# Writing out the last five slots, moving constant loads and border work

## What is computed

```python
x = _layernorm(x + _L0_attn_ref(x, ...))                 # linear attention with cos/sin features
x = _layernorm(x + _L0_xattn_ref(x, ctx_2048, lens, ...)) # rmsnorm, W_in, plus a table row per patch
x = _layernorm(x + _L0_ffn_ref(x, weight, bias))         # both operands rounded to 6-bit floats in blocks of 32
```

## Time and profile before

| | us |
|---|---|
| median of 3 runs | 1659.92 (1659.71 to 1660.7) |
| the profiled execution | 1660.41 |
| its span, first to last instruction | 1658.6 |
| mean granted clock, share of 2.4 GHz | 0.984 |

### The profile page before, as it was taken

How to read it: one execution, slowest core, us unless ns; L and a number is a source line. 1 busy time by engine, 2 the same in 40 slices (tenths; PEclk the granted TensorE clock), 3 DMA queues, 4 the chain that set the end, 5 groups by cost and what they waited for, 6 DMA issues and landing times. The chain is left out here.

```text
span 1658.6 us, 29661 instructions
## 1 busy us (share of the span) xinstructions
PE 1588.7 (96%) x11188; PEld 1122.3 (68%) x11188; DVE 1188.5 (72%) x1831; ACT 1115.1 (67%) x1454; POOL 711.1 (43%) x668
## 2 busy tenths in 40 slices
PE   6999999999999999999999999988699999999995
PEld 4756675676676667667666756754478888888884
DVE  5677667758757766875776676888587777777873
ACT  5597678668667767866876776678145656565654
POOL 2033105303411520440341053346178878897886
PEclk8999999999999999999999999999799999999998
DMA  4100202200210220220022022001612222222211
GB/s 169 52 26 1 78 1 78 77 1 26 77 52 1 77 77 2 67 86 2 2 77 77 1 78 77 27 26 51 162 32 83 83 77 83 82 84 78 74 52 51
DMA packets 49175, 95.75 MB, mean 58 GB/s; under 512 B 3552, under 2 KB 3872, under 8 KB 49056
## 3 DMA queue, kind: packets, MB, share of 16 engines
q1 hardware_dynamic: 38944, 76.29, 14.5%
q10 hardware_dynamic: 10112, 17.69, 2.9%
HBM read 60.38 MB, written 33.59 MB: 57 GB/s over the span
## 5 line engine op out<-in xcount | busy, mean ns | idle before, releaser
L764 DVE SCALAR_TENSOR_TENSOR feat<-feat,phases 128x1024 f32<-128x1024 f32 x256 | 300.8, 1216 | 177.0 <-ACT feat L657 176.9
L657 ACT ACTIVATE feat<-phases 128x1024 f32<-128x1024 f32 x256 | 248.3, 1024 | 147.1 <-PE phases L510 125.5
L664 ACT ACTIVATE feat<-feat 128x1024 f32<-128x1024 f32 x256 | 271.7, 1062 | 67.6 <-DVE feat L764 58.8
L383 POOL TENSOR_TENSOR xt_hi<-xt_raw,singles 128x512 fp32r<-128x512 f32 x60 | 69.0, 1180 | 526.6 <-PE bank L502 491.9
L670 ACT ACTIVATE feat<-feat 128x1024 f32<-128x1024 f32 x256 | 255.7, 1045 | 5.1 <-DVE feat L771 5.1
L771 DVE TENSOR_SCALAR feat<-feat 128x1024 int32<-128x1024 int32 x256 | 198.7, 780 | 45.7 <-ACT feat L664 45.1
L396 POOL TENSOR_TENSOR res<-res,bo_all 128x512 f32<-128x512 f32 x60 | 72.1, 1226 | 182.2 <-DMA res<-x 182.1
L598 PE MATMUL kv_sum<-feat,kv_cols 128*32 128x512 f32 x1024 | 124.3, 603 | 0.0
L572 PE MATMUL kv_sum<-feat,v 128*32 128x256 f32 x2048 | 123.8, 382 | 0.0
L500 PE MATMUL bank<-xt_hi,win_hi 128*128 128x512 f32 x256 | 108.7, 425 | 8.5 <-DVE win_lo L713 8.5
L1232 ACT ACTIVATE xs<-xs,shift,rstd 128x512 f32<-128x512 f32 x96 | 71.4, 806 | 67.3 <-POOL shift L1107 67.3
(11 more groups left out here) (204 smaller groups left out, 3678.7 us busy)
## 6 DMA issues: line engine op xcount, KB each, us to landing
normed<-res SPq DMA_DIRECT2D x32, 513.0 KB, 4.2
xt_raw<-xT SPq DMA_DIRECT2D x15, 1024.0 KB, 7.1
res<-x SPq DMA_DIRECT2D x30, 512.0 KB, 4.1
xs<-normed SPq DMA_DIRECT2D x24, 513.0 KB, 3.9
out<-xs ACTq DMA_DIRECT2D x24, 512.0 KB, 2.8
feat<-normed SPq DMA_DIRECT2D x8, 513.0 KB, 3.8
out<-feat ACTq DMA_DIRECT2D x8, 512.0 KB, 2.8
xt_raw<-ctx SPq DMA_DIRECT2D x8, 256.0 KB, 3.4
```

The lines of the kernel that those rows point to most:

```text
L657: act.activation(feat[2 * (w % 2) + p][:, 0, :], phases[:, 2 * p:2 * p + 2, :].rearrange("p h n -> p (h n)"), ACT.Identity, bias=ROUND).th ...
L664: act.activation(f[:, 1, :], f[:, 0, :], ACT.Sin, scale=-TWO_PI).then_inc(sin_done, 1)
L764: dve.scalar_tensor_tensor(f[:, 0, :], f[:, 0, :], ROUND, phases[:, 2 * p:2 * p + 2, :].rearrange("p h n -> p (h n)"), ALU.subtract, ALU.s ...
```

## The change

It has these parts:

1. SP issues the constant loads, after the weights and ahead of the second chunk of x. DVE makes `lens_f` in `weight_peaks`, near the end of the first part.
2. The DVE steps of the weight rounding stand one phase earlier (cos 2 to cos 7), and POOL runs `residual_weight` right behind `quantise_weight`, before the powers of that batch.
3. The powers have five steps. DVE makes one combined variance after the moments, the norm waits for the first power only, and the store waits for all.
4. The table of batch 0 is made in the first part: the new steps `context`, `table` and `parts` stand between the last output products.
5. In the second part `lin` and `ffn` do the eight matmuls with the high part first. They wait for ACT's high part, and only the last four wait for DVE's low part.
6. The last slots are a list of their own, `closing_steps`, with five slots. Slot 0 normalises the last pair alone, `ffn` results are normalised one slot later, the added bias is a step on POOL, and for the last pair DVE does the scaling and all of the rounding (`by_vector`).

```diff
@@ attention_steps, tail list
-        15: [..., norm(0, 0), norm(0, 1), ("ends",), W(1, 0),
-             ("repeats",), W(1, 1), W(1, 2), W(1, 3), stats(1), norm(1, 0), norm(1, 1)],
+        15: [..., norm(0, 0), norm(0, 1), ("ends",), W(1, 0),
+             ("repeats",), W(1, 1), ("context",), W(1, 2), W(1, 3), stats(1), ("table",), norm(1, 0), norm(1, 1), ("parts",)],
@@ SP
             def store(k, last=False):
+                sp.wait_ge(ln_step, LN_STEPS * (k + 1))
...
                         sp.dma_start(stage[m], w.rearrange("(k p) o -> p k o", p=P)).then_inc(w_in[m], 16)
+                    for to, of in const_loads:
+                        sp.dma_start(to, of).then_inc(const_in, 16)
                     load_xt(1)
@@ POOL, powers
-                pool.wait_ge(moments_done, k + 1)
-                step(1, pool.tensor_tensor(shifted, var, eps[:, 0, :], ALU.add))
-                step(2, pool.tensor_tensor(rstd, shifted, half_power[:, 0, :], ALU.pow))
...
+                pool.wait_ge(var_ready, k + 1)
+                pool.tensor_tensor(scale, spread_var, half_power[:, 0, :], ALU.pow).then_inc(ln_step, 1)
+                pool.tensor_tensor(shifted, var, eps[:, 0, :], ALU.add).then_inc(ln_step, 1)
+                pool.tensor_tensor(root, spread_var, half_power[:, 1, :], ALU.pow).then_inc(ln_step, 1)
+                pool.wait_ge(ln_step, base + 3)
+                pool.tensor_tensor(rstd, shifted, half_power[:, 0, :], ALU.pow).then_inc(ln_step, 1)
+                pool.wait_ge(ln_step, base + 4)
...
+                pool.tensor_tensor(res[:, :, RMS_COL:RMS_COL + 1]..., root, rstd, ALU.mult).then_inc(ln_step, 1)
@@ POOL, tail and last
-                    residual_weight(i - 1)
                     powers(2 * i - 2)
+                    pool.wait_ge(squared, 1)
+                    pool.tensor_tensor(shifted_square, mean_square, rms_eps, ALU.add).then_inc(context_scaled, 1)
+                    pool.wait_ge(context_scaled, 1)
+                    pool.tensor_tensor(context_inv, shifted_square, minus_half, ALU.pow).then_inc(context_scaled, 1)
                     powers(2 * i - 1, last=True)
...
                     quantise_weight()
+                    residual_weight(i)
                 powers(2 * i - 1)
@@ PE, ACT and DVE, the new steps of the first part
+                    elif kind == "table":
+                        pe.wait_ge(patch_ready, 1)
+                        pe.matmul(out_part[0], kept.decay[:], patch, start=True, stop=True).then_inc(table_done, 1)
...
+                    elif kind == "context":
+                        act.wait_ge(kept.context_in, 16)
+                        act.wait_ge(win_split, KD)
+                        act.activation(squares, context, ACT.Square, scale=DCTX ** -0.5, accum_out=mean_square).then_inc(squared, 1)
...
+                    elif kind == "context":
+                        dve.wait_ge(context_scaled, 2)
+                        dve.wait_ge(constants_in, 16 * 3)
+                        dve.scalar_tensor_tensor(patch, context[:, 0:D], context_inv, kv_cols[0:PATCHES, 1, :], ALU.mult, ALU.mult).then_inc(patch_ready, 1)
...
-            for to, of in const_loads:
-                act.dma_start(to, of).then_inc(const_in, 16)
...
-            dve.wait_ge(const_in, CONSTS)
-            dve.tensor_copy(lens_f[:], lens_i[:]).then_inc(lens_ready, 1)
@@ second part, first slot and closing slots
-            [("select",), ("turn", 0), ("patch",), ("count",), ("table",), ("choose",), ("turn", 1), ("means",), ("norms",)],
+            [("select",), ("turn", 0), ("count",), ("turn", 1), ("choose",), ("means",), ("norms",)],
...
+        [("quant", -3), ("lin", -1, 0), ("lin", -1, 1), ("means", 0), ("norms", 0), ("scale", -2), ("ffn", -4, 0), ("ffn", -4, 1),
+         ("back", -3, 0), ("back", -3, 1)],
+        [("bias", -3), ("quant", -2), ("means", 0), ("norms", 0), ("scale", -1), ("ffn", -3, 0), ("ffn", -3, 1),
+         ("back", -2, 0), ("back", -2, 1)],
+        [("bias", -2), ("means", 0), ("norms", 0), ("quant", -1), ("ffn", -2, 0), ("ffn", -2, 1), ("back", -1, 0), ("back", -1, 1)],
+        [("bias", -1), ("means", 0), ("norms", 0), ("ffn", -1, 0), ("ffn", -1, 1)],
+        [("means", 0), ("norms", 0)],
@@ PE, second part
-                        product(b[:], turn_hi[t], turn_lo[t], win_hi, win_lo, False)
+                        freed(last_use)
+                        wait(pe, hi_ready, i * hi_order.n + hi_place(mode, ("turn", k, t)) + 1)
+                        high_product(b[:], turn_hi[t], win_hi, win_lo)
+                        freed(place(mode, ("turn", k, t)))
+                        low_product(b[:], turn_lo[t], win_hi, False)
```

164 lines of the change are left out of this document (105 added, 59 removed).

## The result

The changed kernel takes 1649.55 us (median of 4 runs, 1647.99 to 1650.35), the kernel before beside it 1659.82 (1658.61 to 1660.7). The ratio is 0.9921, with a 95% interval of 0.9905 to 0.9937. The forecast was 1642 with a range of 1631 to 1651. The time lies inside the range, but 7.5 us above the number and 2.5 above the band of the likeliest case (1637 to 1647). The profiled execution took 1648.75 us with a span of 1646.9, against 1660.41 and 1658.6, so its span is 11.7 us shorter. The forecast had 17.9.

The account below looks back on a forecast made before the run. PE was taken as the bound, busy for 96% of the span, with its idle time in four places. Terms 10.2 - 0.8 + 4.0 + 4.5 = 17.9 us off 1660.4 gave 1642.5, forecast as 1642, range 1631 to 1651.

Parts of the forecast that it names:

- start (phase 2 on PE): First part's start: without the wait for constants, phase 2 comes at 41.2 instead of 51.47, 10.2 us gained.
- border, up to the barrier: End of the first part: first store 4.6 us earlier, but DVE's wait for the context moves the barrier 0.8 us later.
- second part, its beginning: First slots of the second part: `lin` starts earlier (2.6 us) and waits for low parts shrink (1.4), 4.0 us gained.
- closing slots: Last slots of the second part: the last pair's rows come earlier and the clock stays up, 4.5 us gained.
- DVE has the query split and a slow first cosine in between: Start, before phase 2: DVE frees the bank of V(0, 3) late, for which 1.4 us were added.
- the start gains half: Rival at the start: the second chunk or the clock holds PE, 5.5 instead of 10.2 us, time 1647; chance 0.12.
- The second chunk's cap: Start: the second chunk of x, issued 1.3 us later, costs nothing until its delay passes 2.9 us.
- The wait in DVE's queue: Border: DVE waits in order for the context landing at 1173.5, with the last sums, statistics, moments and norm queued behind.
- Moving `residual_weight`: Border: POOL's work a phase earlier slows DVE's masks there, moving 1.7 us a phase from phases 14 and 15 to 8 and 9.
- The divided product: Second part's beginning: matmuls with the high part fill 0.7 us of each of two 1.0 us waits, 1.4 gained.
- for the case that POOL leaves DVE alone: Closing slots: 0.5 us added to the 4.0 gained, for DVE working on the last pair undisturbed by POOL.
- No gain between the four places: Between start, border, second part's beginning and last slots PE has no gaps, so savings on other engines are worth nothing.

Follow-up runs that it names:

- e2: The changed kernel with the query weight's low parts made directly behind V(0,0), ahead of phase 0's sines: median 3.0 us less than the changed kernel, phase 2 at 42.02.
- e3: The changed kernel with the context step behind the last two output products and their statistics, and the table's step behind the last norms: 5.2 us less than the changed kernel.
- e4: The changed kernel with POOL's work on the residual weight put back behind the last bias: median 1.3 us over the changed kernel's, with overlapping intervals.
- e7: The changed kernel with every second-part product again waiting for the low parts before its first matmul, the new matmul order kept: median 1648.80 us.
- e8: The changed kernel with the closing slots of the kernel before, keeping the divided product: median 1.2 us over the changed kernel's.
- e6: The changed kernel with the last pair scaled and quantised by POOL: from the peak of pair -3 to the end 61.05 us, 4.8 more than the changed kernel.
- e9: The changed kernel with DVE's scaled context of the second batch earlier, ahead of the first turn in the fourth slot: median 3.0 us less, with overlapping intervals.

## Why the prediction was right in direction and off in size

The ledger of the two profiled executions, in the prediction's terms:

```
                              forecast   measured
start (phase 2 on PE)             10.2       5.0
border, up to the barrier         -0.8       0.7
second part, its beginning         4.0       3.0
closing slots                      4.5       3.0
sum                               17.9      11.7
```

The border holds 2.0 us gained between phase 2 and phase 15, and the beginning 0.4 lost in E.

- *Start: the mis-sized term, 10.2 for 5.0.* The mechanism was right: the constants' wait went, the value weights are split at 13.6, and PE is in phase 0 at 15.8. The failed step is the estimate that "DVE has the query split and a slow first cosine in between", priced at 1.4 us for one bank. Moved earlier, the query split met POOL's split of the second chunk and took twice as long. PE waited 2.91 us and then ran at half the clock. e2 takes the subtractions out of the meeting and has phase 2 at 42.0, 0.8 from the forecast's 41.2. The rival "the start gains half" had the right size and named the clock as one cause, but not this wait. I had looked for what was late next on PE, SP and POOL, and not for what POOL would now be doing beside DVE, although the rows of phase 15 showed its price.
- *The second chunk's cap: right.* It was issued at 14.94, 3.6 us later than before, more than the 1.3 I had counted. It landed at 23.30, 0.3 later. The Trainium skill, DMA: Bandwidth & Descriptors, Issuing engines are not separate DMA queues, says that all issuers share the same 16 DMA engines. From this the prediction took that the landing hardly moves, and the trace agrees.
- *Border: -0.8 for 0.7.* The first store was to come 4.6 us earlier, counted without the start's gain, and came 4.8 earlier. The landing was to be 14.4 us behind it and was 13.9. The agreement is partly luck: from phase 2 to phase 15 the changed kernel gained 2.0, and this stretch scatters by up to 3.8 between kernels with the same steps. In the last batch, phase 9 came 1.9 us sooner behind phase 2 than before (forecast about 1), and PE's waits in phases 8 and 9 fell from 2.32 and 1.51 us to 1.89. The wait in DVE's queue took 4.1 back, as forecast in kind (5.4). e3 shows that it was avoidable: two entries of the list in another order give 4.9 us.
- *Moving `residual_weight`:* the masks were to lose in phases 8 and 9 what 14 and 15 gain. e4 shows 1.0 us for it at phase 14 and 1.2 behind phase 15 against 0.6 of waiting in phase 9, less than the 1.7 a phase that I had moved.
- *Beginning: 4.0 for 3.0.* The first `lin` was to gain 2.6 and gained 3.7. The divided product was to add 1.4. It did shorten the two waits (1.05 and 0.98 us to 0.42 and 0.34), but from the first peak to the fourth the changed kernel is 0.3 slower than before, and 0.4 went in E. That step is wrong: e7 does without it and is no slower there. The table's matmul waits a few slots further on and takes whatever comes early.
- *Closing: 4.5 for 3.0.* The number hides three things. DVE's rows of the last pair were to be ready 1.5 us earlier, and PE did take them that much earlier (39.2 for 40.6 from the start of F). This was partly luck, since DVE's scaling took 3.4 us beside POOL, where at most 2.9 were counted, and its five steps 6.1 for 5.5. The early start and the clock were to give 2.5, and the last product did end 2.3 sooner behind that point, at a clock of 0.98. But this is the divided product's doing, since e8 has it with the old list. I had given 1.8 of it to the list and 0.7 to the product. The mis-sized terms are the chain behind PE's end, which "stays 9.1 us" and became 9.87, since ACT has pair -2 to normalise and to store first, and the 0.5 added "for the case that POOL leaves DVE alone", which did not come. And e6 shows that the list needs DVE's work on the last pair, else it costs 4.2 us against e8.
- *No gain between the four places: right.* E is the same within 0.4 us. What moved inside B lies in the last batch, where the weight's steps were moved.

## What to carry to other kernels

When a step is moved, look at what the other engines do at its new time, not only at what it waits for: DVE's subtractions at 0.68 us became 1.4 to 1.5 beside POOL, and one step placed ahead of the meeting gave 3 us back. In a hand-written list that all engines walk, a step that waits for a DMA goes behind everything that is ready (4.9 us here for one line). A gain in one slot lasts only up to the next wait that doesn't move with it, so follow it to the first one whose releaser stands outside the change. And a long wait with a low clock behind it is no proof of a cost: look whether the next wait grows when it goes, as in the closing slots.

## What the runs showed of the hardware that was not expected

**The same wait, two clocks.** PE waited 2.88 to 2.91 us for the keys at the start in all nine profiles with the changed start. In three of them (e4, e7, e9) the clock stayed at 1.00. In five it fell for some 3.4 us, and in the changed kernel for some 6.8: in the five windows of 2 us from 34 to 44 us it had 0.84, 0.50, 0.50, 0.50 and 0.95, where e3 had 0.97, 0.50, 0.68, 1.00 and 1.00. The first two windows are of the changed kernel, behind the keys and behind a wait of 1.89 us in phase 9 (1092.6):

```profile
...
36.00:38.00 2.00, 2.00 (x5) 1.63 (x6) 0.53 (x1) 0.36 (x1) 0.00 (x0) 0.50 0.00 0
1094.00:1096.00 2.00, 2.00 (x6) 1.52 (x6) 2.00 (x2) 1.63 (x2) 2.00 (x3) 0.50 0.00 0
...
```

In e4, PE's wait and the window behind it:

```profile
...
36.53 0.50 PE L511 MATMUL bank<-wf_hi,xt_hi 128*128 128x512 f32 x1 [2.91 <-DVE keys L802]
...
38.00:40.00 2.00, 2.00 (x10) 1.59 (x9) 0.36 (x1) 0.00 (x0) 0.00 (x0) 1.00 0.00 0
...
```

In e3, the window behind the wait of 1.89 us in phase 9:

```profile
...
1094.00:1096.00 2.00, 2.00 (x11) 1.60 (x10) 2.00 (x2) 1.63 (x2) 2.00 (x3) 1.00 0.00 0
...
```

This is 1.2 GHz in the one and 2.4 GHz in the other, with the same instructions ahead. From the end of that wait to the end of A the three take 10.0 us, the five 11.3 to 11.5 and the changed kernel 12.8, so the clock makes 0, some 1.4 or 2.8 us in A. It makes 1.5 us in phase 9. From phase 9 to phase 10 six of the thirteen profiles take 10.5 us and seven 8.4 to 9.0 (8.4 is e4, whose wait was 1.27). What decides between them was not tried. It means that one profiled execution can't tell what a wait of 2 to 3 us costs here, nothing, or about as much again behind it. Differences of 1 to 3 us between two profiles can come from this alone.

**Who pays when DVE and POOL meet.** DVE's four subtractions took 5.73 us for 2.48 in e2, so DVE lost 3.2 us. POOL's two passes beside them took 5.38 and 5.82. The kernel before had 4.87 and 5.48, so POOL lost 0.9 against it. But in e2, with other work of DVE beside them, they took 5.15 and 5.95, which is 0.1 less in all. What these subtractions alone cost POOL is therefore not shown, only that DVE lost most.
